# The last layer's bias: added to x in place by VectorE instead of by a matmul

## The reference

```
# layer 0, by condition
out_nr  = gelu(x @ w1_nr  + b1_nr)  @ w2_nr  + b2_nr       # condition 0
out_tsr = gelu(x @ w1_tsr + b1_tsr) @ w2_tsr + b2_tsr      # condition 1
h       = gelu(x @ w1_sr  + b1_sr)                         # condition 2, 512 wide
h       = gelu(h @ w2_sr  + b2_sr)
out_sr  = h @ w3_sr + b3_sr
y = x + out                                                # zeros for any other condition
z = layernorm(y) * gamma + beta
# layer 1, by domain
hidden = gelu(z @ down_W.T + down_b)
hidden = hidden @ expert_W[domain].T + expert_b[domain] + domain_emb[domain]
u = hidden @ up_W.T + up_b + z
result = layernorm(u) * ln_gamma + ln_beta
```

## Time and profile before

| what | value |
|---|---|
| median of 3 runs | 278.47 us (277.82 to 278.58) |
| span of the profiled execution | 275.1 us |
| median less that span | 3.4 us |
| PE busy | 259.9 us (94%) |
| PEld busy | 241.4 us (88%) |
| DVE busy | 210.0 us (76%) |
| ACT busy | 208.2 us (76%) |
| POOL busy | 149.7 us (54%) |
| mean granted TensorE clock | 0.994 |

### The profile page before, as it was taken

The page is one execution under the profiler, slowest core; times in us unless marked ns, Lnnn a source line. Parts: engine busy times, 40 slices in busy tenths (PEclk is TensorE's granted clock), DMA queues, the critical chain, the costliest instruction groups (busy, mean ns, idle before and its releaser), DMA issues.

```text
span 275.1 us, 8498 instructions
## 1 busy us (share of the span) xinstructions
PE 259.9 (94%) x2151; PEld 241.4 (88%) x2152; DVE 210.0 (76%) x726; ACT 208.2 (76%) x491; POOL 149.7 (54%) x171
## 2 busy tenths in 40 slices
PE   7998999999999998899999999999999999999880
PEld 7687889999999997799999999999999999999670
DVE  7897422544944944989898899998898989999884
ACT  3588687687687686688888887888888878888750
POOL 3332574454656655555566565565665655658562
PEclk9999999999999999999999999999999999999997
DMA  6372751011121121132332424243332424232133
GB/s 189 83 251 47 154 100 33 9 44 29 41 69 47 33 72 48 33 91 67 86 83 70 100 64 117 72 104 76 77 88 67 105 75 116 69 92 58 42 97 79
DMA packets 45326, 21.84 MB, mean 79 GB/s; under 512 B 37831, under 2 KB 43575, under 8 KB 45304
## 3 DMA queue, kind: packets, MB, share of 16 engines
q1 hardware_dynamic: 42612, 16.39, 25.0%
q0 software_dynamic: 1536, 4.20, 4.6%
q10 hardware_dynamic: 1156, 1.00, 1.3%
HBM read 11.69 MB, written 8.65 MB: 74 GB/s over the span
## 4 chain that ended last, share of the span: by engine, by line
PE 84%; DVE 8%; issue 3%; ACT 2%; DVEq 0%; POOL 0%; ACTq 0%; POOLq 0%
PE ps_h L1108 20%; PE ps_z L1185 10%; PE ps_u L1237 10%; PE ps_d L1252 6%; PE ps_z L1190 5%; PE ps_t L1207 5%; PE ps_u L1143 5%; PE ps_z L1143 5%; PE ps_z L1173 4%; PE ps_t L1298 3%; PE ps_t L1301 3%; PE ps_t L1299 3%; PE ps_u L1074 1%; DVE st L725 1%; DVE n L738 1%
## 5 line engine op out<-in xcount | busy, mean ns | idle before, releaser
L497 POOL TENSOR_TENSOR h_lo<-h,h_hi 128x256 fp32r<-128x256 f32 (+1 forms) x75 | 69.7, 930 | 76.2 <-ACT h L911 76.2
L504 POOL TENSOR_TENSOR rs<-ve,minus_half 128x4 f32<-128x4 f32 (+1 forms) x38 | 41.0, 1078 | 32.6 <-DVE ve L714 32.0
L911 ACT ACTIVATE h_hi<-ps_h,per_feature_sb 128x256 fp32r<-128x256 f32 x84 | 38.1, 479 | 22.9 <-PE ps_h L1108 22.8
L702 DVE BATCH_NORM_STATS2 st<-ps_z 128x6 f32<-128x256 f32 x66 | 24.9, 418 | 33.8 <-PE ps_z L1190 33.8
L918 ACT ACTIVATE zn<-ps_z,nm,rs 128x256 f32<-128x256 f32 x66 | 33.5, 561 | 8.8 <-DVE nm L718 8.6
L531 POOL DMA_INDIRECT out<-o,out_rows_now x32 | 34.2, 1068 | 8.2 <-issue 5.6
L961 ACT ACTIVATE yt<-ps_t,per_feature_sb 128x256 f32<-128x256 f32 x66 | 34.0, 573 | 5.9 <-PE ps_t L1207 5.8
L911 ACT ACTIVATE h<-ps_h,per_feature_sb 128x256 f32<-128x256 f32 x84 | 38.0, 481 | 0.0
L1237 PE MATMUL ps_u<-table_hi,stack 128*128 x132 | 35.9, 303 | 0.0
L1237 PE MATMUL ps_u<-table_lo,stack_hi 66*128 x132 | 33.1, 282 | 0.0
L1185 PE MATMUL ps_z<-last_hi,h_hi 128*128 (+1 forms) x132 | 32.6, 281 | 0.3 <-ACT h_hi L911 0.3
(11 more groups left out here) (157 smaller groups left out, 685.7 us busy)
## 6 DMA issues: line engine op xcount, KB each, us to landing
x<-in_x_feat SPq DMA_DIRECT2D x130, 64.0 KB
out<-o SPq DMA_DIRECT2D x65, 64.0 KB
table_hi<-table_hi SPq DMA_DIRECT2D x2, 576.0 KB, 6.3
last_sb<-in_last_w SPq DMA_DIRECT2D x1, 768.0 KB, 5.0
w_sr_sb<-in_w_sr SPq DMA_DIRECT2D x1, 512.0 KB, 4.0
w_sr_sb<-in_w_sr ACTq DMA_DIRECT2D x1, 512.0 KB, 4.8
w_two_sb<-in_w_two SPq DMA_DIRECT2D x1, 512.0 KB, 5.6
out<-o,out_rows_now POOLq DMA_INDIRECT x32, 2.6
```

The source lines that it names most:

```text
L497: pool.tensor_tensor(dst, full, high.bitcast(F32), ALU.subtract).then_inc(ready, 1)
L504: pool.tensor_tensor(RS[p][:, norms, :], VE[p][:, norms, :], half_of_two[:, norms, :], ALU.pow).then_inc(rstd, 1)
L911: ins = act.activation(dst[:, m, :], src[m], ACT.Gelu, bias=COL[:, bass.ds(col + m, 1)])
```

## The change

The bias is no longer a matmul. In the front VectorE compares the kind of each slot's first position with the number of the partition (`SLOT_KIND`, 4 x 36), and TensorE multiplies the bias rows by it: `SLOT_B` then holds, for every slot, the bias as a column per feature half. In each step VectorE adds that column to `XF` in place, by two instructions of 128x256 (`add_bias`), once x_hi and x_lo have been made from it; it raises `x_sum`, for which the residual's transposes now wait instead of x_lo. The adds stand behind `finish` and ahead of `stack_low`; those of slots 0 and 1 are in the front. `LBH`, its halves, `ones2`, the memset, the two DMAs and the product of line 1173 are gone.

```diff
+        SLOT_KIND = sb("slot_kind", [KINDS, POS // G])
+        SLOT_B = sb("slot_bias", [P, KC, POS // G])
@@ sync
-            sp.wait_ge(s_lb, 1)
-            sp.wait_ge(s_lbh_zero, 1)
-            for row, half in enumerate((LB_HI, LB_LO)):
-                sp.dma_start(LBH[row:row + 1, :].bitcast(F32), half[:, :].bitcast(F32)).then_inc(s_lb_low, 16)
@@ gpsimd
-            pool.memset(LBH[:, :].bitcast(F32), 0.0).then_inc(s_lbh_zero, 1)
@@ vector
-            step(dve.memset(ones2[:, :].bitcast(F32), 0.0))
-            dve.memset(ones2[0:2, :].bitcast(F32), 1.0)
...
             dve.tensor_copy(IDS[:, 0, 0:POS], H0[0:1, 1, 0:POS]).then_inc(s_ids, 1)
+            dve.tensor_scalar(SLOT_KIND[:, :], ZP[1][0:KINDS, 0, 0:POS:G], seq_no[0:KINDS, :], None,
+                              ALU.is_equal).then_inc(s_slot_kind, 1)
...
-            dve.wait_ge(s_lb_in, 16)
-            step(dve.tensor_copy(LB_HI[:, :], LB[:, :]))
-            dve.tensor_tensor(LB_LO[:, :], LB[:, :], LB_HI[:, :].bitcast(F32), ALU.subtract).then_inc(s_lb, 1)
+            def add_bias(slot, p):
+
+                for c in range(KC):
+                    ins = dve.tensor_scalar(XF[p][:, c, :, :], XF[p][:, c, :, :], SLOT_B[:, c, bass.ds(slot, 1)],
+                                            None, ALU.add)
+                ins.then_inc(x_sum, 1)
+
+            dve.wait_ge(s_slot_b_ps, 1)
+            dve.tensor_copy(SLOT_B[:, :, :], ZP[1][:, :, POS:POS + POS // G]).then_inc(s_slot_b, 1)
+            dve.wait_ge(s_slot_b, 1)
+            dve.wait_ge(x_lo, 1)
+            add_bias(0, 0)
...
                         input_low(1, 1)
+                    dve.wait_ge(x_lo, 2)
+                    add_bias(1, 1)
...
                     finish(slot, i - 2 if p == 0 else i - 1, q, where)
+                for slot in on_slot(g, -2, where):
+                    dve.wait_ge(x_lo, slot + 1)
+                    add_bias(slot, p)
                 for slot in on_slot(g, 1, where):
                     stack_low(slot, q, False)
@@ tensor
-            pe.matmul(ZP[1][0:1, 0, 0:POS], kind_no[:, :], place[:, :], start=True, stop=True)
+            pe.matmul(ZP[1][0:KINDS, 0, 0:POS], kind_no[:, :].to_broadcast([P, KINDS]), place[:, :], start=True, stop=True)
...
+            pe.wait_ge(s_slot_kind, 1)
+            pe.wait_ge(s_store_ids, 1)
+            pe.wait_ge(s_lb_in, 16)
+            for c in range(KC):
+                ins = pe.matmul(ZP[1][:, c, POS:POS + POS // G], LB[:, c * P:c * P + P], SLOT_KIND[:, :],
+                                start=True, stop=True)
+            ins.then_inc(s_slot_b_ps, 1)
...
-                    pe.wait_ge(x_lo, g + 2)
+                    pe.wait_ge(x_sum, g + 2)
...
-            def last_layer(kind, highs, lows, p, first):
-
-                if first:
-                    pe.wait_ge(s_lb_low, 32)
-                pe.matmul(ZP[p][:, :, :], ones2[:, :],
-                          LBH[:, bass.ds(kind * H, H)].unsqueeze(1).to_broadcast([P, TT, H]),
-                          start=False, stop=False)
+            def last_layer(kind, highs, lows, p):
```

More of the change, by code:

```diff
@@ L89, in conditioned_layers @@
         LB = sb("last_b_sb", [KINDS, H])
-        LB_HI = sb("last_b_hi4", [KINDS, H], F32R)
-        LB_LO = sb("last_b_lo4", [KINDS, H], F32R)
-        LBH = sb("last_b_hi", [P, KINDS * H], F32R)
+        SLOT_KIND = sb("slot_kind", [KINDS, POS // G])
+        SLOT_B = sb("slot_bias", [P, KC, POS // G])
         IDI = sb("ids_i", [P, 2], I32)
@@ L98, in conditioned_layers @@
         gelu_warm = sb("gelu_warm", [P, 1])
-        ones2 = sb("ones2", [P, P], F32R)
         seq_no = sb("seq_no", [P, 1])
@@ L191, in conditioned_layers @@
         s_ct_in = sem("s_ct_in")
-        s_lb = sem("s_lb")
-        s_lb_low = sem("s_lb_low")
+        s_slot_kind = sem("s_slot_kind")
+        s_slot_b_ps = sem("s_slot_b_ps")
+        s_slot_b = sem("s_slot_b")
         s_fold = sem("s_fold")
@@ L198, in conditioned_layers @@
         s_stack = sem("s_stack")
-        s_lbh_zero = sem("s_lbh_zero")
         ld_x = [sem(f"ld_x{p}") for p in range(2)]
@@ L206, in conditioned_layers @@
         x_lo = sem("x_lo")
+        x_sum = sem("x_sum")
         x_used = sem("x_used")
@@ L1323, in finish_sr @@
                 weights_ready(where, g, "last")
-                last_layer(SR, lambda: None, lambda: pe.wait_ge(h2_lo, g + 1), p,
-                           where == HEAD and g == 0)
+                last_layer(SR, lambda: None, lambda: pe.wait_ge(h2_lo, g + 1), p)
                 with pe.If(g + 1 < b_sr):
@@ L1335, in finish_other @@
                     weights_ready(where, g, "last")
-                    last_layer(kind, lambda: pe.wait_ge(h1_hi, g + 1), lambda: pe.wait_ge(h1_lo, g + 1), p,
-                               where == HEAD and g == 0)
+                    last_layer(kind, lambda: pe.wait_ge(h1_hi, g + 1), lambda: pe.wait_ge(h1_lo, g + 1), p)
                 start_two(g, 1 - p, where)
```

## The result

The change makes the kernel slower: median 293.4 us (292.06 to 294.55, 4 runs) against 278.14 us (277.16 to 278.58, 4 runs) of the kernel before, ratio 1.0579 (1.0543 to 1.0616). The forecast was 292.7 us. All ratios here compare undisturbed executions only: in some executions of seven of the twelve kernels, the one before included, some 6 to 8 us come on top (e1's trace is of such a one), and a kernel's median lies higher than its ratio says where many of its executions are like that.

A forecast was written before the change was run, and what follows sets the result against it. VectorE was to become the second stage's bound, TensorE's matmul stream looking like the only one before: 12.3 + 0.5 + 0.7 + 0.9 - 0.2 = 14.2 us on the 275.1 span, 289.3, plus 3.4: 292.7 us; own range 288 to 298, overall 280 to 302.

The forecast's parts named there:

- the hold of `nm`: Second stage: x_lo ahead of `rs` makes h_lo late, which holds `nm`; eats the 0.24 us slack and 0.05 more.
- The add: VectorE, per slot: two in-place adds of 0.34 us each, overlapping by 0.09, so a slot pays 0.51 us.
- the prediction's other estimate: VectorE's add by the Trainium skill's table: 0.19 us, a slot paying some 0.3 us less than taken.
- The rival of held adds: GpSimd's DMA_INDIRECT holds VectorE's adds, 0.3 to 0.4 us a second-stage step; 301.8 us in all; chance 0.15.
- TensorE's 0.22 buys nothing: Second stage: removing the bias product frees 0.22 us on TensorE, without gain because VectorE becomes the bound.
- The faster rival: The adds hide on VectorE, TensorE keeps the bound and gives 7.6 us less 0.9: 271.8 us; chance 0.09.
- The SR stage: First nine slots: adds ahead of stack_low delay L1237; +0.1 us a step, 8 steps, +0.7.
- the stall: SR step, at L1237: 0.51 us of adds less 0.18 spare, 0.33 us, from which TensorE's 0.23 is taken.
- The head: Ahead of the steps: one-hot, two small float32 products, first adds; +0.9 us, between 0.3 and 2.5.
- The end: At the drain: the last product gives 0.2 us back, as no add runs there.
- The step of change: Between SR and second stage: some 0.5 us more, one slot's adds.
- the signs: Second stage: step 6.6 to 6.75, VectorE over 9.5 tenths, TensorE some 89%, `nm` 0.6 to 0.7; SR steps 10.5.

The follow-up runs named there:

- e1: The changed kernel without VectorE's 66 adds, last layer's bias left out: 277.71 us against 276.46 of the kernel before, ratio 1.0041.
- e5: The changed kernel with VectorE's two center instructions split around `ve`, so `rs` starts ahead of x_lo: 288.71 us, ratio 1.0419 to the kernel before.
- e3: The changed kernel with GpSimd's second h_lo of a step waiting until `nm` is done: 299.19 us, ratio 1.0803 to the kernel before.
- e7: The changed kernel with the adds behind stack_low instead of ahead of it: 296.81 us, ratio 1.0687 to the kernel before.
- e4: The changed kernel with a zero-weight product of 512 columns in the bias product's old place: median 298.56 us, the profiled execution 294.25, no ratio.
- e6: The changed kernel with center split around `ve` and without the two adds, bias left out: 274.66 us, ratio 0.990 to the kernel before.
- e2: The changed kernel with one add of two per slot, only feature half 0 getting its bias: 284.77 us, ratio 1.030 to the kernel before.
- e8: The changed kernel with center split around `ve` and ScalarE making the adds from the third slot on: 278.54 us against 277.63 before, ratio 1.003.
- e10: The changed kernel with center split, adds of SR slots by VectorE, the others by ScalarE: median 279.96 us, ratio 1.0051 to the kernel before.

## Why the prediction was right, point by point

- **VectorE becomes the bound of the second stage, the hold of `nm` eats the slack: shown.** x_lo at +0.10, `rs` 1.45, `nm` 0.64, h_lo ending at +2.40 and `o` at +2.41, where 2.42 and 2.43 were worked out. e1 shows the hold without adds, e5 that it is worth 0.3 us in a step in which it goes. Its first formulation was too narrow: not `nm` but whatever comes next with two inputs is held (e3), and a cast too (e5).
- **The add, 0.34 us and 0.26 from start to start: right for the first one** and far from the 0.19 of the prediction's other estimate. The second takes 0.42 in nearly every step: both start inside the indirect store (164.69 to 165.90), the first isn't held by it, the second ends 0.09 behind its end. So a slot pays 0.60, not 0.51; `o` starts 0.03 later, not 0.05, and that is the gap between 6.67 and 6.74. e5's second stage and e7, whose adds lie outside, have 0.35 for both. The rival of held adds (0.3 to 0.4 a step) was the right mechanism at a fifth of its size. Over 22 steps it made 1.5 us.
- **"TensorE's 0.22 buys nothing" in the second stage: shown** by e4 (6.740 with a product again), and e6 goes beyond: with neither adds nor hold on VectorE the step falls by 0.02 of the 0.22, about half of it lost to the wait for h_hi. The faster rival's 7.6 us was never there; some 2 of it were, in the SR stage.
- **The SR stage: right path and sign, mis-sized.** 0.1 a step was said, 0.25 measured. Two terms of the stall were short. The adds took 0.60, not 0.51, so stack_hi ends at +5.53 instead of +4.94; and before the change only 0.11 was spare, not 0.18, as the expert product's load can follow stack_hi by 0.12 and followed by 0.23. So the product moved by 0.48 (+5.17 to +5.65), not 0.33; less TensorE's 0.23 that is 0.25. The transposes' wait for the add is a second edge, left out of the prediction; here it isn't the last one, and e7 shows how hard it is when it is. e6 confirms the 0.2 that TensorE gives. (Eight steps of 0.1 are also 0.8 and not the 0.7 of the sum.)
- **The head: +0.9 said, +1.1 up to the fourth SR step, and the agreement is luck.** In the change's trace the granted clock fell to 0.77 and 0.81 in the head (rows below). e4 has the change's head and even the product, and its clock stayed at 1.00; its first SR step takes 10.11 us instead of 11.38, and its fourth SR `ve` is at 60.47, 0.3 behind the kernel before. As far as two traces tell, some 0.8 of the 1.1 is the lower clock, which nobody forecast, and the head's own work costs nearer 0.3. The forecast didn't see either that adds in the head and the first SR steps would be held by an h_lo of 128x512: the second add of three pairs takes 1.4 us (from 19.47, 42.10 and 52.39). One of the pairs:

```profile
41.84 1.65 DVE L691 TENSOR_SCALAR x<-x,slot_bias 128x256 f32<-128x256 f32 x2
...
41.96 1.37 POOL L491 TENSOR_TENSOR h_lo<-h,h_hi 128x512 fp32r<-128x512 f32 x1 [0.23 <-ACT h L919]
```

- **The end: right.** The +0.5 measured holds the twenty-second step with adds, the one that begins at 263.17 and whose 0.60 the forecast counted with the second stage; -0.1 is left where -0.2 was said. The step of change was +0.6 for 0.5. Of the signs, TensorE was to be some 89% busy in the second stage and was 93% (27.89 of 30).
- **The closeness of the total is partly luck as well.** The span grew by 16.2 us where the sum said 14.2: 1.1 of that is the second stage with the end, 0.8 the SR stage with the head. Against it, the 3.4 us added to the span were 1.7 too many: the profiled execution took 293.04 us for a span of 291.3. They were the distance from the median to the span of one execution, which need not be a middling one.

## What to carry to other kernels

Work moved off the busiest engine is worth only what the next bound leaves: count the receiver's slack in one step, start to start, before the price of the operation. A wait that goes can change an order between two engines that share SBUF, and a small instruction then pays for a large one of another engine. When a product is removed, ask which wait it covered.

## What the runs showed of the hardware

- VectorE and GpSimd meet not only at semaphores. VectorE's instructions with two SBUF inputs, and casts and in-place adds with one, are held if they start while GpSimd's two-input h_lo runs: `nm` 0.13 to 0.64 or 1.2 us, `o` 0.47 to 0.83, a cast 0.22 to 0.74, an add 0.35 to 1.4. The add that started 0.12 ahead of h_lo (41.84) was not held: 0.35.
- Between x_lo and `rs` it matters who starts first. Wherever x_lo starts ahead, by 0.25 us or next to nothing, `rs` ends 0.86 to 0.91 behind the end of x_lo (1.45 us in the change, 1.59 in e2's step at 117.55). Wherever x_lo starts behind `rs`, by 0.76 down to 0.01 us, `rs` takes 1.01 to 1.04 and x_lo 0.68 to 0.73, inside it: a `rs` that has started doesn't hold x_lo.
- Of two adds inside the indirect store the first lasts 0.34, the second 0.42 (0.55 once), always to 0.09 behind the store's end. The store takes 1.04 in the second stage before and 1.21 in the change, as in the SR steps before: both times it starts within the first `o`. Why the first add isn't held was not found.
- In the head of the change the granted clock fell to 0.77 and 0.81 for two stretches of 4 us, with TensorE idle for 1.03 of 4 us in the one before and 1.05 in the first of the two; before the change it was 1.00 there. A mean of 0.77 is 46% of the stretch at 1.2 GHz and the rest at 2.4, one of 0.81 is 38%. e3, e7 and e8 fell alike (0.75 to 0.82 in the same two stretches); e4 didn't (last two rows), nor did e5, though its TensorE was idle for 2.04 us from 24 to 28. So what idle time brings it down isn't shown.

```profile
20.00:24.00 4.00, 2.97 (x26) 2.73 (x24) 3.96 (x5) 2.96 (x6) 0.70 (x1) 1.00 0.31 68
24.00:28.00 4.00, 2.95 (x16) 2.75 (x17) 3.77 (x7) 3.93 (x10) 2.38 (x2) 0.77 0.30 67
28.00:32.00 4.00, 4.00 (x27) 3.81 (x27) 2.13 (x9) 2.12 (x7) 2.74 (x3) 0.81 0.95 206
```

```profile
24.00:28.00 4.00, 3.15 (x23) 2.90 (x24) 3.73 (x7) 3.93 (x10) 2.24 (x2) 1.00 0.42 94
28.00:32.00 4.00, 4.00 (x34) 3.82 (x34) 2.89 (x9) 1.86 (x6) 3.68 (x3) 1.00 0.98 206
```

The first SR step took 11.38 us instead of 9.40, and the two behind it 0.36 and 0.23 less than before. The three traces that fell like it have 11.28 to 11.42, e4 and e5 10.11 and 9.85. Over whole executions of the change: the one with a mean clock of 0.991 took 292.06 us, the three with 0.981 to 0.984 took 293.04 to 294.55. No two executions of the change itself, one with the fall and one without, were profiled, so the price of the fall stays an estimate. Nor was it settled why e1, e2, e5 and e10 alternate between two lengths of step; the rows show what is held or waited for in each, not what starts the rhythm.
